# Routed experts with four row buffers and four result buffers, and a finer-grained end

## The reference

```python
probs = jax.nn.softmax(x @ gate_w.T, axis=-1)                 # 8 experts
routing_weights, selected = jax.lax.top_k(probs, 2)
routing_weights = routing_weights / (routing_weights.sum(axis=-1, keepdims=True) + 1e-20)
combine = jnp.sum(jax.nn.one_hot(selected, 8) * routing_weights[..., None], axis=1)
out = jax.nn.silu(x @ shared_gate.T) * (x @ shared_up.T) @ shared_down.T    # shared expert, 704 wide
g = jnp.einsum('nh,eih->nei', x, expert_gate)                               # experts, 352 wide
u = jnp.einsum('nh,eih->nei', x, expert_up)
y = jnp.einsum('nei,ehi->neh', jax.nn.silu(g) * u, expert_down)
out = out + jnp.einsum('neh,ne->nh', y, combine)
```

## Time and profile before

| | |
|---|---|
| Median of three runs | 1648.87 us (1646.89 to 1652.2) |
| The profiled execution's own time | 1656.13 us |
| Span of its trace | 1654.4 us |
| PE busy | 1607.7 us (97%) |
| Mean granted TensorE clock | 0.995 |
| Last down products of the shared expert | about 1309 to 1367 us of the span |
| Routed tiles | about 1364 to 1641 us |

### The profile page before, as it was taken

The page is one execution under the profiler, slowest core; times in us unless marked ns, Lnnn a source line. Parts: engine busy times, 40 slices in busy tenths (PEclk is TensorE's granted clock), DMA queues, the critical chain, the costliest instruction groups (busy, mean ns, idle before and its releaser), DMA issues.

```text
span 1654.4 us, 24639 instructions
## 1 busy us (share of the span) xinstructions
PE 1607.7 (97%) x8400; PEld 1389.9 (84%) x8401; DVE 898.9 (54%) x1541; ACT 585.3 (35%) x996; POOL 687.8 (42%) x567
## 2 busy tenths in 40 slices
PE   7999999999999999999999998999999999999996
PEld 5888888888888888888888886788999978998895
DVE  4777656676656677656666657334552472222221
ACT  4454443344343443434433443333111312332231
POOL 4666554555535556536456443202100003333342
PEclk9999999999999999999999999999999999999998
DMA  7776454577576677666677784654430017778752
GB/s 279 283 283 229 172 190 168 201 284 270 220 259 249 241 279 260 235 254 232 257 272 258 300 312 158 225 170 126 177 108 3 7 63 233 234 201 260 187 90 41
DMA packets 82906, 342.16 MB, mean 207 GB/s; under 512 B 8512, under 2 KB 8512, under 8 KB 77184
## 3 DMA queue, kind: packets, MB, share of 16 engines
q1 hardware_dynamic: 69792, 303.18, 50.1%
q0 software_dynamic: 13024, 37.79, 9.5%
HBM read 220.89 MB, written 120.05 MB: 206 GB/s over the span
## 4 chain that ended last, share of the span: by engine, by line
PE 76%; DMA 7%; issue 6%; POOL 6%; DVE 3%; ACT 1%; SPq 0%; DVEq 0%; POOLq 0%; ACTq 0%
PE bank L337 24%; PE bank L339 24%; PE bank L338 24%; DMA out<-rows,ids_e 6%; POOL pre_split L572 2%; PE bank L1615 1%; POOL key_sums L621 1%; POOL probs L611 1%; PE bank L1710 1%; PE bank L1737 1%; POOL key_sums L619 1%; POOL key_sums L617 1%; DMA rows<-x_rows,ids_e 1%; DMA rows<-xs 1%; PE bank L1805 0%
## 5 line engine op out<-in xcount | busy, mean ns | idle before, releaser
L611 POOL TENSOR_TENSOR probs<-probs,causal 128x256 f32<-128x256 f32 x126 | 91.5, 747 | 405.9 <-ACT probs L801 405.9
L339 PE MATMUL bank<-store,wqk 128*128 128x512 f32 x512 | 202.1, 395 | 0.0
L337 PE MATMUL bank<-store,wqk 128*128 128x512 f32 x512 | 201.9, 394 | 0.1
L338 PE MATMUL bank<-store,wqk 128*128 128x512 f32 x512 | 201.9, 394 | 0.0
L1146 DVE SCALAR_TENSOR_TENSOR resid<-bank,factor,resid 128x512 f32<-128x512 f32 x256 | 189.1, 740 | 10.0 <-PE bank L339 9.9
L1140 DVE TENSOR_TENSOR q_lo<-bank,q_hi 128x512 fp32r<-128x512 f32 x64 | 44.3, 692 | 193.3 <-ACT q_hi L841 193.3
L799 ACT ACTIVATE probs<-bank 128x512 f32<-128x512 f32 x189 | 85.8, 527 | 157.5 <-PE bank L339 157.4
L1154 DVE TENSOR_TENSOR p_lo<-probs,p_hi 128x1280 fp32r<-128x1280 f32 x63 | 120.6, 1914 | 2.2
L572 POOL TENSOR_TENSOR pre_split<-pre_raw,pre_split 128x1528 fp32r<-128x1528 f32 x34 | 120.8, 3553 | 0.0
L718 POOL DMA_INDIRECT out<-rows,ids_e x39 | 61.7, 1583 | 134.7 <-ACT rows L881 85.0
L711 POOL DMA_INDIRECT rows<-x_rows,ids_e x39 | 38.2, 979 | 188.2 <-DVE ids_e L1442 137.4
(11 more groups left out here) (327 smaller groups left out, 4241.5 us busy)
## 6 DMA issues: line engine op xcount, KB each, us to landing
pre_parts<-pre_split SPq DMA_DIRECT2D x34, 1528.0 KB, 6.5
wqk<-wqk_parts SPq DMA_DIRECT2D x96, 512.0 KB
pre_raw<-pre SPq DMA_DIRECT2D x34, 764.0 KB, 7.7
store<-wv_parts SPq DMA_DIRECT2D x12, 2048.0 KB, 9.5
wo<-wo_parts SPq DMA_DIRECT2D x48, 512.0 KB, 6.7
expert_w<-pre_parts SPq DMA_DIRECT2D x8, 2816.0 KB
wqk_parts<-wqk SPq DMA_DIRECT2D x16, 1024.0 KB, 5.6
expert_w<-pre_parts SPq DMA_DIRECT2D x8, 1536.0 KB
```

The costliest lines, as they stand in the source:

```text
L337: nc.tensor.matmul(out_ap, a_hi, b_hi, start=first, stop=False)
L338: nc.tensor.matmul(out_ap, a_hi, b_lo, start=False, stop=False)
L339: return nc.tensor.matmul(out_ap, a_lo, b_hi, start=False, stop=last)
L611: nc.gpsimd.tensor_tensor(diagonal, diagonal, causal[:, :, :], ALU.mult).then_inc(S["masked"], 1)
```

## The change

It has six parts. (1) `rows` holds four gathered tiles instead of two, and gathers run six ahead instead of four. (2) Results go to four buffers in `x3_early`, which is free by then, instead of two in `rows`; `y_copy_e` waits for add(g - 4). ACT's loop for routed tiles is written out, PE's is rolled by four. (3) A gather now also waits until the last gather that used its semaphore has landed. (4) In the shared expert's last products `down_s` waits for each of the three low parts where it reads it, and `shared_add` stands ahead of `aT_low_s` on DVE; down(g) of the routed tiles waits for its two low parts one by one. (5) up(0) and T(1) move into `down_s(15)`, ahead of its last chunk, and DVE makes `xT_lo` of tile 1 ahead of `shared_add(15)`. (6) At the end down(37) moves between the gate and the up product of tile 38, down(38) writes another bank, and the wait for the last addition moves from POOL to SP.

```diff
@@ SP
             for e in range(2, EXPERTS):
                 load_expert(e)
+            sp.wait_ge(S["e_added"], 16 * ETILES)
@@ POOL
                 if g < 2:
                     pool.wait_ge(S["s_xT_ready"], TILES - 1 + g)
                 else:
-                    pool.wait_ge(S["e_xT_ready"], g - 1)
-                nc.gpsimd.indirect_dma_start(rows[:, g % 2, :], None, x3_rows, bass.IndirectOffsetOnAxis(ids_e[:, g:g + 1], 0)).then_inc(S[f"e_row{g % 2}"], 16)
+                    pool.wait_ge(S[f"e_row{g % 2}"], 16 * (g // 2))
+                if g >= E_ROWS:
+                    pool.wait_ge(S["e_xT_ready"], g - E_ROWS + 1)
+                nc.gpsimd.indirect_dma_start(rows[:, g % E_ROWS, :], None, x3_rows, bass.IndirectOffsetOnAxis(ids_e[:, g:g + 1], 0)).then_inc(S[f"e_row{g % 2}"], 16)
...
-            for g in range(4):
+            for g in range(E_AHEAD):
                 gather(g)
             pool.wait_ge(S["stored"], 16 * TILES)
             for g in range(ETILES):
-                if g + 4 < ETILES:
-                    gather(g + 4)
+                if g + E_AHEAD < ETILES:
+                    gather(g + E_AHEAD)
                 add_rows(g)
-            pool.wait_ge(S["e_added"], 16 * ETILES)
@@ ACT
+            def y_copy_e(g):
+                act.wait_ge(S["e_y"], g + 1)
+                if g >= E_ROWS:
+                    act.wait_ge(S["e_added"], 16 * (g - E_ROWS + 1))
+                nc.scalar.activation(x3_early[:, g % E_ROWS, :], bank[e_bank(g)][:, :], ACT.Copy).then_inc(S["e_y_out"], 1)
+            def step_e(g):
+                if g == ETILES - 1:
+                    y_copy_e(g - 1)
+                act.wait_ge(S["e_up"], g + 1)
+                if g:
+                    act.wait_ge(S["e_aT_ready"], g)
+                nc.scalar.activation(act_sb[:, 0:INNER], bank[0][:, 0:INNER], ACT.Silu).then_inc(S["e_silu"], 1)
+                if g < ETILES - 1:
+                    xT_high("e", g + 1)
+                    if g:
+                        y_copy_e(g - 1)
+                if g == 0:
+                    act.wait_ge(S["s_y"], TILES - 1)
+                aT_high("e", g)
@@ DVE
+                if not last:
+                    xT_low(ph, g + 1)
                 if ph == "e" and first:
                     shared_add(TILES - 1)
-                if not last:
-                    xT_low(ph, g + 1)
...
+            shared_add(FULL_STEPS + 2)
             aT_low_s(FULL_STEPS + 4)
-            shared_add(FULL_STEPS + 2)
             hot_places(0)
@@ PE, down_s
-                pe.wait_ge(S["s_aT_lo"], 3 * (t + 1))
...
+                    if c in (0, KC):
+                        pe.wait_ge(S["s_aT_lo"], 3 * t + 1 + c // KC)
                     triple(to[:, :], hi[:, c, :], lo[:, c, :], sh_down_hi[:, c, :], sh_down_lo[:, c, :], c == 0, False)
+                pe.wait_ge(S["s_aT_lo"], 3 * t + 3)
+                if SC - 1 in between:
+                    between[SC - 1]()
@@ PE, the order of the calls
+            def first_up_e():
+                pe.wait_ge(S["route_e_done"], 1)
+                e_up(0, place(0), first=True)
+                transpose_rows_e(0, 1)
...
+                if t == TILES - 1:
+                    between = {2: first_rows_e, SC - 1: first_up_e}
+                down_s(t, between)
             e_step(0, 0, first=True)
             pe.wait_ge(S["s_y_out"], TILES)
             e_step(0, 1, second=False)
-            by_twos(pe, e_step, 2, ETILES - 1)
-            e_step((ETILES - 1) // 2, (ETILES - 1) % 2, last=True)
-            e_down(ETILES - 1, place(ETILES - 1), True)
+            by_fours(pe, e_step, 2, ETILES - 2)
+            last = ETILES - 1
+            transpose_rows_e(last // 4, last % 4)
+            e_down(last - 2, place(last - 2), True)
+            transpose_act("e", last - 1)
+            at = place(last - 1)
+            e_up(last, place(last), between=lambda: e_down(last - 1, at, True))
+            transpose_act("e", last)
+            e_down(last, place(last), False, to=e_bank(last))
```

More of the change, by code:

```diff
@@ L295, in by_twos, with by_fours, e_bank @@
                 step(stop // 2, 0)
+        def by_fours(engine, step, start, stop):
+            first, end = -(-start // 4), stop // 4
+            for g in range(start, 4 * first):
+                step(g // 4, g % 4)
+            with engine.Fori(first, end) as i:
+                for j in range(4):
+                    step(i, j)
+            for g in range(4 * end, stop):
+                step(g // 4, g % 4)
+        def e_bank(g):
+            return XT if g == ETILES - 1 else YB
         TAIL_BANKS = ((7, 0, 1, 7), (7, 1, 2, 3))
@@ L312, in build @@
         SH_PIECES = 2 * KC + 4
+        E_ROWS, E_AHEAD = 4, 6
         LAST_PARTS = ((0, SEQ), (SEQ, SEQ), (2 * SEQ, 2 * P))
@@ L971, in _ @@
             xT_high("e", 0)
-            feed_forward("e", begun=True)
+            for g in range(ETILES):
+                step_e(g)
+            y_copy_e(ETILES - 1)
         @block.vector
@@ L1711, in transpose_rows, with up @@
                 last.then_inc(S[f"{ph}_xT_ready"], 1)
-            def up(ph, g, products, first):
+            def up(ph, g, products, first, between=None):
                 pe.wait_ge(S[f"{ph}_xT_lo"], g + 1)
@@ L1717, in up @@
                 for j, (hi, lo) in enumerate(products):
+                    if j and between:
+                        between()
                     for k in range(KC):
@@ L1720, in up, with down @@
                 last.then_inc(S[f"{ph}_up"], 1)
-            def down(ph, g, hi, lo, second, between=None):
-                pe.wait_ge(S[f"{ph}_aT_lo"], len(aT_parts(ph)) * (g + 1))
+            def down(ph, g, hi, lo, second, between=None, to=YB):
                 if second:
                     pe.wait_ge(S[f"{ph}_y_out"], g)
+                parts = aT_parts(ph)
                 for c in range(NCH[ph]):
@@ L1729, in down @@
                         between()
-                    last = triple(bank[YB][:, :], aT_hi[0:w, c, :], aT_lo[0:w, c, :], hi(c, w), lo(c, w), c == 0, c == NCH[ph] - 1)
+                    for n, (c0, _) in enumerate(parts):
+                        if c == c0:
+                            pe.wait_ge(S[f"{ph}_aT_lo"], len(parts) * g + n + 1)
+                    last = triple(bank[to][:, :], aT_hi[0:w, c, :], aT_lo[0:w, c, :], hi(c, w), lo(c, w), c == 0, c == NCH[ph] - 1)
                 last.then_inc(S[f"{ph}_y"], 1)
@@ L1806, in transpose_act_s, with down_s @@
                 nc.tensor.transpose(aT_s(t, SC - 1, SC)[:, 0, :], of[:, SHARED - P:SHARED], ident[:, :]).then_inc(S["s_aT_ready"], 1)
-            def down_s(t, between=None, late=None):
-                pe.wait_ge(S["s_aT_lo"], 3 * (t + 1))
+            def down_s(t, between={}):
                 if t:
@@ L1829, in slot_table, with place, e_up, e_down @@
                 last.then_inc(S["table_ready"], 1)
-            def transpose_e0():
-                pe.wait_ge(S["s_y_out"], TILES - 1)
-                transpose_rows("e", 0, 0)
+            def place(g):
+                return pe.value_load(place_e[0:1, bass.ds(g, 1)], min_val=0, max_val=1)
+            def e_up(g, p, first=False, between=None):
+                products = [[lambda k, at=part + c * INNER: expert_w[:, bass.ds(p, 1), at + 2 * INNER * k:at + 2 * INNER * k + INNER].rearrange("p a n -> p (a n)")
+                             for part in (0, UP)] for c in range(2)]
+                up("e", g, products, first, between)
+            def e_down(g, p, second, between=None, to=YB):
+                down("e", g, *[lambda c, w, at=part: expert_w[0:w, bass.ds(p, 1), at + c * D:at + c * D + D].rearrange("p a n -> p (a n)")
+                               for part in (2 * UP, 2 * UP + DOWN)], second, between, to)
+            def transpose_rows_e(i, j):
+                pe.wait_ge(S[f"e_row{j % 2}"], 32 * i + 16 * (j // 2) + 16)
+                for k in range(KC):
+                    last = nc.tensor.transpose(bank[XT][:, k * P:k * P + P], rows[:, j % 4, k * P:k * P + P], ident[:, :])
+                last.then_inc(S["e_xT_ready"], 1)
+            def e_step(i, j, first=False, second=True):
+                g = 4 * i + j
+                following = []
+                if first:
+                    following.append(place(g + 1))
+                else:
+                    p = place(g - 1)
+                    transpose_rows_e(i, j + 1)
+                    e_down(g - 1, p, second, lambda: following.append(place(g + 1)))
+                transpose_act("e", g)
+                e_up(g + 1, following[0])
+            def first_rows_e():
+                pe.wait_ge(S["s_y_out"], TILES - 1)
+                transpose_rows_e(0, 0)
+            def first_up_e():
+                pe.wait_ge(S["route_e_done"], 1)
+                e_up(0, place(0), first=True)
+                transpose_rows_e(0, 1)
             pe.wait_ge(S["sh_zeroed"], 1)
```

54 lines of the change are left out of this document (12 added, 42 removed).

## The result

The median after the change is 1643.69 us (1641.02 to 1645.07, nine runs), that of the kernel before in the same rounds 1648.87 us (1646.89 to 1653.1). The ratio is 0.9959, with an interval of 0.9947 to 0.9972: 6.8 us less, between 4.6 and 8.7. The prediction was 1636.1 us and 12.8 us less. The median stands 0.2 us above the upper end of the range; by the ratio, 0.9959 of 1648.87 us, the kernel stands at 1642.1 us, inside it.

What follows compares the result with a forecast made beforehand. PE, busy 97% of 1654.4 us, was taken as the bound, with the chain of additions under its routed tiles. 3.2 + 0.8 + 7.9 - 1.3 - 0.9 + 3.1 = 12.8 us less gave a median of 1636.1 us, range 1631 to 1643.5.

Steps and rivals of the forecast that it cites:

- I move the difference over to the median unchanged: Whole kernel: the 12.8 us summed for the profiled span were taken off the median of 1648.87 us as well.
- I take the whole 7.9 us, half clock included: Routed tiles, T(3) to T(38): deeper row and result buffers win back all 7.9 us lost there; bounds 4 and 7.9.
- Most of the stalls stand only in the profile: Rival, routed tiles: timed executions lose only 1 us there, or the stalls stay; 6.9 us missing, 1643.0 us; chance 0.17.
- The shared expert and the first tile: Shared expert's last products and first routed tile: finer waits, swapped additions and moved matmuls gain 3.2 and 0.8 us.
- The slack at the table: DVE's last table value is done 0.73 us before PE asks for it; at most 1 us lost, none taken.
- The buffers' mechanism: Routed tiles: gathers six ahead and four result buffers cover late rows and slow additions; ACT's wait for `out` near nothing.
- additions come more than 7 us apart: Sign on POOL's queue in the routed tiles that would show the prediction wrong.
- The reckoning of the margin: Result buffers: 3.3 us of falling back plus 9.3 us of slow additions, 12.6 us, fit the 13.4 us more of allowed lag.
- The end on PE: Last tile: Silu and multiplication of tile 38 are no longer covered by down(37), so PE ends 1.3 us later.
- the chain of additions: End of the routed tiles: the additions come last, at 1635.9 instead of 1635.0 us, costing 0.9 us; bounds 0 and 4.
- PE will idle no less there, so I leave that as it is: Last product on PE: it stays at the lower clock for 3.3 us, behind idle time; no gain or loss taken.
- The drain: End on POOL: with the wait on SP, its 7.75 us drain begins at the last addition's issue, 3.1 us sooner.

Runs made afterwards that it cites:

- e_two_two: The changed kernel with two row buffers, gathers four ahead and two result buffers, as before: 1646.62 us, ratio 0.9983 to the kernel before.
- e_two_small: The changed kernel with two row and two result buffers, loading only 64 columns of each weight of experts 2 to 7: 1642.61 us, ratio 0.9956.
- e_swap_back: The changed kernel with the shared expert's six additions behind the low parts again and one wait for all low parts: 1646.72 us, ratio 0.997.
- a_again: The changed kernel, unedited, timed and profiled once more: 1643.73 us, ratio 0.9964 to the kernel before.
- e_tail: The changed kernel with the last tile's order as before, down(37) behind both up products of tile 38: 1641.08 us, ratio 0.9954.
- e_poolwait: The changed kernel with the wait for the last addition back on POOL instead of SP: 1645.85 us, ratio 0.9979 to the kernel before.
- b_again: The kernel before, unedited, profiled a second time and timed against itself: 1647.99 us, ratio 1.0001.
- e_rows4: The changed kernel with four row buffers and gathers six ahead, but two result buffers as before: 1647.76 us, ratio 0.998.
- b_third: The kernel before, unedited, profiled a third time in a single execution: 1648.77 us.

## Why the prediction was right in kind and off in size, point by point

**The failed step** is the sentence "I move the difference over to the median unchanged", for one term: "I take the whole 7.9 us, half clock included". As a statement on that profile the term is right to 0.1 us (242.04 to 234.15). As a term of the median it is too large. Three profiles of the kernel before lose 7.9, 0.7 and 1.2 us in the stretch, and in timed executions four buffers of each kind bring 3 to 4 us by the ratios (e_two_two against the changed kernel). On these middle values that is 4 to 5 of the 6.0 us that are missing between 12.8 and 6.8; the size in timed executions is known to some 3 us only. The lower bound of the term was 4, for a wrong reason (that half of the stalls stay; none did).

**The rival that came nearest** is "Most of the stalls stand only in the profile", which had 1643.0 us with 1 us lost in timed executions; the ratios say 3 to 4, the two later profiles 0.7 and 1.2. Its sign was in the rows: the profiled time was 7.3 us above the median and the stretch had lost 7.9. Against it stood that the chain of additions binds with or without a profiler. e_two_small shows what was wrong with that: the chain binds only where the loads of weights fall on it badly, and one execution is one draw. The profiler does not cause it either: two other profiled executions don't show it, and one timed run was as long.

**The shared expert and the first tile**, 3.2 + 0.8 us. The profile gives 4.0 to T(3). Against all three profiles of before (T(3) at 1383.90, 1382.98, 1383.07) and both of after (1379.88, 1380.08) it is 3.3. The swap and the finer waits carry it, e_swap_back shows, with 2.9 us at T(0) and 1.0 to 1.8 by the ratios. Of the two stretches of the first tile 0.26 and 0.37 us are left, 0.3 forecast. The slack at the table is 0.47 us (last value at 1348.76, asked for at 1349.23) and was 0.73: no stall, as taken. Not foreseen were the 0.48 us that T(0) waits for its gathered row, since PE comes there earlier and the gather doesn't.

**The buffers' mechanism** was right: ACT's wait for `out` near nothing (3.0 us), no slow step, slow additions hidden in the margin. The sign "additions come more than 7 us apart" did not come: additions 13 to 31 are 6.4 us apart on average. The reckoning of the margin (12.6 of 13.4 us) has the slow additions in both of its terms, in the mean of 6.87 us and once more by themselves, so it was less narrow than it looked. The runs point to both halves being needed, which the prediction treated as two separate reasons and never weighed one without the other.

**The end on PE**, +1.3 us, and **the chain of additions**, +0.9 us: together 2.2, measured 1.2 in the profile and 1.3 in a_again (16.97). The first term was right: down(38) starts 12.00 us behind T(38), where it was 10.88 before. The second did not come: the last addition waited for ACT, not for addition 37. But the floor is close, as forecast. Where PE is earlier (e_tail starts down(38) 10.7 us behind T(38), and at the higher level), the chain comes last, with additions 5.3 to 5.7 us apart. The last product ran at the lower level as assumed, with its matmuls 0.43 us apart, but that was luck: "PE will idle no less there, so I leave that as it is" does not decide it. The kernel before has the higher level there in both later profiles, behind the same 1.61 us, and 15.3 and 15.7 us to the last addition. Against these the end of the changed kernel is as long where it has the higher level too (15.4 to 15.5).

**The drain**, -3.1 us: -3.2 in the profile and 3.3 in e_poolwait. The Trainium skill, "VectorE: DVE Perf Modes", "The DRAIN you can't avoid", has about 12 ns for such a drain on every engine, by which the moved wait would bring nothing. Every profile here shows 7.75 us or a little more on POOL (7747 ns where it waited first), so the measurement decides against it. In the changed kernel DVE's took 595 ns and ACT's 627, and only SP's, 7 ns, is in its range.

**The sum over medians.** By the ratios against 0.9959 the parts are 3.3 (wait on SP), 1.8 (swap and finer waits) and 4.0 (buffers), less the 1.2 us of the profile at the end of PE: 7.9 us, inside the 4.6 to 8.7 of the whole. Against 0.9964 they are 2.5, 1.0 and 3.1, and the sum is 5.4 us. The 0.8 us of the first tile, which no run undid, is in neither. So the ratios bear out the sum, but not the size of any one part closely. By the profiles the fixed part, span less stretch, fell from 1411.6 (mean of three) to 1406.6 (mean of two), 5.0 us, where 4.9 was forecast. Had b_again been the profile at hand, the same method would have given 0.7 + 4.9 = 5.6 us and 1643.3 for the median.

**What stays open**: why some executions run the last product, or the stretch near 1019 us, at the lower granted clock and others do not; whether the last tile's order matters in the median; and how large the buffers' share is there. The profile of e_two_two had its last product at the higher level and those of the changed kernel at the lower, so the ratios may show the buffers smaller than they are.

## What to carry to other kernels

A stall that hangs on transfers has the size that one execution drew. Where the profiled time lies above the timed runs by about as much as the stall, take a second profile before its size goes into a forecast for the median, or discount it by that distance. Where one in-order queue carries both what feeds a loop and what drains it, deepen the buffers on both sides or on neither: one side alone gave nothing measurable here. And a wait for the last transfer belongs on an engine whose own end is cheap, so that a long drain elsewhere runs beside it.

## What the hardware showed unexpectedly

POOL's drain takes 7.75 us without a transfer in flight and 7.75 to 8.0 with one, and runs beside it. An addition of 128 rows started as little as 5.3 us after the one before when no weights were loaded (e_tail, the last two), and up to 9 to 12 us after it beside the loads of weights, though those use SP's queue. "DMA: Bandwidth & Descriptors" of the Trainium skill, "Anatomy of one DMA", gives 2.6 us for its 256 KB by my estimate. The trace doesn't agree: the chain of the changed kernel has 4.66 us for addition 37:

```profile
1624.51 4.66 DMA out<-x_early,ids_e
```

The granted clock of the last product does not follow from PE's idle time ahead of it. Behind 1.17 and 1.26 us the changed kernel had matmuls 0.43 us apart, the lower level, and e_two_two, e_rows4 and e_two_small had them 0.23 apart, the higher. Behind a single stretch of 1.61 us the kernel before had the lower level in the earlier trace rows, and the higher one in b_third and in b_again, whose matmuls behind this row start 0.23 us apart:

```profile
1628.73 0.49 PE L337 MATMUL bank<-expert_w,aT_hi 128*128 x1 [1.61 <-DVE aT_lo L1304]
```

A comparison of two single profiles can thus be off by some 1.5 us at this one place.
